# Second layer's attention, first pass over the heads: where the probabilities are multiplied by their reciprocal sum

## The chip, the cores and the metric

The kernel runs on one core of a Trainium2 chip. The metric is the device time of one execution in microseconds. The kernel before took 3354.78 us (median of 3 runs, 3352.99 to 3357.09). A core has five engines that run at the same time, each with its own list of instructions in a fixed order: TensorE (PE: matmuls, and PEld: its weight loads), VectorE (DVE), ScalarE (ACT), GpSimd (POOL) and SyncE (SP, which starts DMAs). They wait for each other by semaphores.

## The reference, cut to what matters

The program is a stack of four layers, each an attention and a feed-forward part. The change touches the attention of the second layer (`layer1_attention` in the code, since layers count from 0). It has two passes over 4 batches of 256 tokens and 16 heads of width 128: self attention over 256 keys, then attention over a context of 512 keys.

```python
def _gqa(q, k, v):
    scale = 1.0 / np.sqrt(q.shape[-1])
    scores = jnp.einsum('bsghd,btgd->bghst', q, k) * scale
    p = jax.nn.softmax(scores, axis=-1)
    return jnp.einsum('bghst,btgd->bsghd', p, v)
...
q = _ln(_fp8_linear_pertensor(ln_out, wq, wq_scale, q_in_scale).reshape(b, s, g, hpg, d), qln_w, qln_b)
k = _ln(_fp8_linear_pertensor(ln_out, wk, wk_scale, k_in_scale).reshape(b, s, g, d), kln_w, kln_b)
v = _fp8_linear_pertensor(ln_out, wv, wv_scale, v_in_scale).reshape(b, s, g, d)
core = _gqa(q, k, v).reshape(b, s, nh * d)
...
catq = _div_clamp_fp8(jnp.concatenate([core, xout], axis=-1), proj_smooth)
return jnp.einsum('bsi,oi->bso', catq, wproj) * (proj_in_scale * proj_w_scale)
```

The softmax of a row is exp(score - row maximum) divided by its sum. The kernel forms the exponentials and their sums, then multiplies the probabilities by the reciprocal of the sum.

## The kernel before, in words

**Slots.** Every engine runs the same loop over slots, `for g in range(FIRST, LAST)`. Slot g is one head of one batch: slots 0 to 63 are the first pass (4 batches of 16 heads, 256 keys), slots 64 to 127 the second (512 keys). The stages of a head are spread over three slots, so that three heads are in flight. In its part of slot g

- PE computes the scores of head g (`scores`, L1597, into banks that the exponentials of head g-1 must have left), transposes the probabilities of head g-1 (`turn`, L1606), does one projection for a later group of four heads (`unit`, L1653 for q and L1661 for k), transposes a normalised projection (`turn_unit`, L1684), projects values (`values`, L1675), weights the values of head g-1 (`weighted`, L1617) and projects the output of head g-2 (`project_out`, L1629).
- DVE takes the row maxima of head g (`maxima`, L1902), rounds the output of head g-2 to the fp8 grid (`quantize_head`: L1920, then `to_e4m3fn`, L1336 to L1342, which ends in `a_cat`), forms the reciprocals of the sums of head g (`reciprocal`, L1907), and takes mean and variance of the projection (`unit`, L1886, L1889, L1896, which ends in `a_head_var`). In slots 3, 4 and 5 of the first three batches, and slot 3 of the fourth, it also rounds the inputs of the next batch (`quantize`, L1864 to L1876, ahead of the next maxima).
- ACT copies the weighted output of head g-2 out of PSUM (`keep_out`, L1734), copies the transposed probabilities of head g-1 (`keep_turned`, L1774), takes the exponentials of head g (`exps`, L1782), normalises the projection of slot g-1 (`norm_unit`, L1742), multiplies the probabilities of head g (`scale`, L1789), and moves transposed projections and values (L1758, L1767). In some slots it starts with four products over weights (`scale_q`, L1717, L1718).
- POOL turns a variance into scale and bias (`coefs`, L1556 to L1561). In some slots it first forms the low part of the q weights (`q_low`, L1567), in others it ends with the split of the output weights (`split`, L1548, L1550).

**Four slots, one group.** Units fall in the slots whose number leaves 2, 3 or 0 when divided by 4, values in those that leave 1. `q_low` falls in slots 0, 4, 45, 49, 53 and 57 of the first pass, `split` in slots 2, 6, 10, 58 and 62.

**Buffers.** Probabilities, reciprocals and maxima have two buffers each. The semaphore `probs_ready` counts the heads whose probabilities are finished; `turn` of head g waits for g+1. In the second pass DVE does the multiplication itself (`normalize`, L1914).

Of the kernel before, what the change touches and what calls it, by code (L numbers as in the profile page):

```python
# [10 lines left out]
ALU = mybir.AluOpType  # L11
# [7 lines left out]
S = 256  # L19
# [4 lines left out]
TB = S // P  # L24
# [71 lines left out]
def rstd_gpsimd(core, g, shifted, rstd, var_ready, rstd_ready):  # L96
    g.wait_ge(var_ready, 1)
    g.tensor_tensor(rstd[:, :], shifted[:, :], core.neg_half[:, 0:NT], ALU.pow).then_inc(rstd_ready, 1)
# [217 lines left out]
def at_least(eng, sem, value):  # L316

    if isinstance(value, int) and value <= 0:
        return
    eng.wait_ge(sem, value)  # L320
# [1024 lines left out]
def layer1_attention(core):  # L1345
# [4 lines left out]
    HPQ, GPQ = 4, 2  # L1350
# [7 lines left out]
    HEADS = PASSES * H  # L1358
    KEYS = (S, C)
    SCORES, TURN, OUT, PROJECT, TURNED, SUM = 0, 2, 3, 4, 6, 7  # L1360
    with ExitStack() as ctx:
# [24 lines left out]
        probs, probs_t = sb("probs", [P, 2, TB, C]), sb("probs_t", [P, 2, CT, S])  # L1386
        neg_max, sums, recip = sb("neg_max", [P, 2, TB]), sb("sums", [P, 2, TB]), sb("recip", [P, 2, TB])
# [14 lines left out]
        scores_full, max_ready, exp_ready, recip_ready = sem("scores_full"), sem("max_ready"), sem("exp_ready"), sem("recip_ready")  # L1402
        probs_ready, turn_full, turn_ready = sem("probs_ready"), sem("turn_full"), sem("turn_ready")
# [11 lines left out]
        def pass_of(quad):  # L1415
            return quad // QUADS // B
# [41 lines left out]
        def halves(g):  # L1458

            return pass_of(g // HPQ) + 1  # L1460
# [16 lines left out]
        def q_columns(n):  # L1477
            return slice(n * QW, (n + 1) * QW)

        def split_count(p, n):  # L1480
            return 2 * (p * QUADS + n + 1)
# [9 lines left out]
        def signed_scale(which):  # L1491
            return 4 if plain(which) else scale_of(which)

        with nc.Block() as block:
# [38 lines left out]
            @block.gpsimd  # L1533
            def _(g):
                rstd_gpsimd(core, g, shifted, rstd, var_ready, rstd_ready)
                g.wait_ge(var_ready, 2)
                g.wait_ge(rstd_ready, 1)
                g.tensor_tensor(rstd[:, :], shifted[:, :], core.neg_half[:, 0:NT], ALU.pow).then_inc(rstd_ready, 1)
                g.wait_ge(rstd_ready, 2)

                def split(p, n):

                    heads = slice(n * HPQ, (n + 1) * HPQ)
                    raw = w_raw[:, n % 2, :, :]
                    g.wait_ge(PROJ_IN[n % 2], 16 * ((p * QUADS + n) // 2 + 1))
                    if p == 1:
                        g.wait_ge(sum_done, (B - 1) * H + (n + 1) * HPQ)
                    g.tensor_copy(w_parts[:, 0, heads, :], raw).then_inc(parts_step, 1)  # L1548
                    g.wait_ge(parts_step, split_count(p, n) - 1)
                    g.tensor_tensor(w_parts[:, 1, heads, :], raw, w_parts[:, 0, heads, :].bitcast(F32), ALU.subtract).then_inc(parts_step, 1)  # L1550

                def coefs(which):
                    i, kind = unit_no[which], signed_scale(which)
                    g.wait_ge(stats_ready, i + 1)
                    at_least(g, normed_ready, i - 3)
                    g.tensor_tensor(head_rstd[:, i % 4, :], head_var[:, i % 4, :], core.neg_half[:, 0:BLOCK], ALU.pow).then_inc(powers_ready, 1)  # L1556
                    g.wait_ge(powers_ready, i + 1)
                    g.tensor_tensor(head_scale[:, i % 4, :], head_rstd[:, i % 4, :], signed[:, 0, kind:kind + 1].broadcast_to([P, BLOCK]), ALU.mult)
                    g.tensor_tensor(head_var[:, i % 4, :], head_rstd[:, i % 4, :], signed[:, 1, kind:kind + 1].broadcast_to([P, BLOCK]), ALU.mult).then_inc(coefs_step, 1)
                    g.wait_ge(coefs_step, i + 1)  # L1560
                    g.tensor_tensor(head_bias[:, i % 4, :], head_moments[:, i % 4, :, 0], head_var[:, i % 4, :], ALU.mult).then_inc(head_coefs, 1)  # L1561

                g.wait_ge(coefs_ready, 1)

                def q_low(p, n):
                    g.wait_ge(q_scaled, p * QUADS + n + 1)
                    g.tensor_tensor(q_w[:, 1, :, q_columns(n)], q_raw[:, n % 2, :, :], q_w[:, 0, :, q_columns(n)].bitcast(F32),  # L1567
                                    ALU.subtract).then_inc(q_parts, 1)

                split_at = {HPQ * n - 2: (0, n) for n in range(QUADS)}  # L1570
                split_at.update({(B - 1) * H + HPQ * n + 10: (1, n) for n in range(QUADS)})
                for slot in range(FIRST, LAST):
                    if slot in q_split_at:
                        q_low(*q_split_at[slot])
                    if slot in unit_at:
                        coefs(unit_at[slot])
                    if slot in split_at:
                        split(*split_at[slot])
# [127 lines left out]
            def _(act):  # L1706
# [15 lines left out]
                for t in range(NT):  # L1722
                    act.wait_ge(token_full, t + 1)
                    for k in range(DK):
                        last = act.activation(ln_t[:, k, t * P:(t + 1) * P], core.bank(4 + t % 4)[:, k * P:(k + 1) * P], ACT.Identity,
                                              bias=cols[:, LNB + k:LNB + k + 1], scale=cols[:, LNW + k:LNW + k + 1])
# [56 lines left out]
                                              bias=neg_max[:, g % 2, t:t + 1], accum_out=sums[:, g % 2, t:t + 1])  # L1783
                    last.then_inc(exp_ready, 1)

                def scale(g):
                    act.wait_ge(recip_ready, g + 1)
                    for t in range(TB):
                        last = act.mul(probs[:, g % 2, t, 0:S], probs[:, g % 2, t, 0:S], recip[:, g % 2, t:t + 1])  # L1789
                    last.then_inc(probs_ready, 1)  # L1790

                for g in range(FIRST, LAST):
                    if g in q_split_at and g > FIRST:
                        scale_q(*q_split_at[g])
                    if 0 <= g - 2 < HEADS:
                        keep_out(g - 2)
                    late = 0 <= g < HEADS and pass_of(g // HPQ) == 0
                    if g - 1 in unit_at and not late:
                        norm_unit(unit_at[g - 1])
                    if 0 <= g - 1 < HEADS:  # L1800
                        keep_turned(g - 1, 0)
                    if 0 <= g < HEADS:
                        exps(g)
                    if g - 1 in unit_at and late:
                        norm_unit(unit_at[g - 1])
                    if late:
                        scale(g)
                    if 0 <= g - 1 < HEADS and halves(g - 1) == 2:
                        keep_turned(g - 1, 1)
                    if g - 2 in unit_at:  # L1810
                        turned(unit_at[g - 2])
                    if g in values_at:
                        keep_values(values_at[g])
# [1605 lines left out]
```

## Time and profile before

| what | value |
|---|---|
| median of 3 runs | 3354.78 us |
| profiled execution, span from first to last instruction | 3349.9 us |
| first pass over the heads, maxima of slot 0 to maxima of slot 64 | 546.42 to 910.12 us, 363.7 us |
| busy in that stretch | PE 308.85, DVE 261.29, ACT 300.93, POOL 114.90 us |
| whole span, busy | PE 85%, DVE 64%, ACT 47%, POOL 11% |

The profiled execution's own time is given only as its span. In the stretch, a slot is 5.7 us long on average. PE and ACT are both busy for more than four fifths of it, so the order of waits, and not the busy share, tells what bounds a slot. The maxima on DVE (L1902) occur once per slot and mark its start.

### The profile page before, as it was taken

The numbers are of one execution on the slowest core, as the hardware profiler recorded it, in microseconds if no ns is written. First come the engines' busy times: TensorE is split into PE (matmuls) and PEld (weight loads), VectorE is DVE, ScalarE is ACT, GpSimd is POOL, SyncE is SP. The second block draws the span as 40 slices with busy tenths as digits, with TensorE's granted clock in tenths as the row PEclk, the third lists the DMA queues.
The fourth block names the chain that finished last, engine by engine and source line by source line (L and its number), as shares of the span: only waits on it lengthen the run. The fifth ranks groups of instructions, "written<-read, shape, count | busy, mean of one in ns | idle before, by whom it ended". The sixth has DMA issues, their size and how long they took to land. (4 is left out here: it accounts for less than half of the span.)

```text
span 3349.9 us, 46674 instructions
## 1 busy us (share of the span) xinstructions
PE 2832.3 (85%) x15008; PEld 1835.0 (55%) x15010; DVE 2142.2 (64%) x5173; ACT 1559.7 (47%) x3247; POOL 376.7 (11%) x675
## 2 busy tenths in 40 slices
PE   7888995898899999638999999836599999857898
PEld 4334664777677777515777777624222223234676
DVE  5675337777666666574444444578999999677432
ACT  4452225888767777452222222213266666624221
POOL 0010004322322212010000000040300000002100
PEclk9798997999999999958999999877699999977899
DMA  1002003000000000003000000001000000020000
GB/s 57 1 2 86 0 4 123 14 1 14 14 8 1 7 1 1 23 11 126 1 1 1 0 0 0 19 5 40 0 1 1 1 1 1 1 96 2 1 0 13
DMA packets 37907, 56.93 MB, mean 17 GB/s; under 512 B 6400, under 2 KB 25792, under 8 KB 36416
## 3 DMA queue, kind: packets, MB, share of 16 engines
q1 hardware_dynamic: 37696, 54.35, 4.8%
q8 instruction: 105, 1.72, 0.2%
q14 instruction: 106, 0.87, 0.1%
HBM read 52.99 MB, written 1.05 MB: 16 GB/s over the span
## 5 line engine op out<-in xcount | busy, mean ns | idle before, releaser
L2754 ACT ACTIVATE a_exps<-psum,a_ln 128x512 f32<-128x512 f32 x512 | 315.0, 684 | 191.0 <-PE psum L2684 191.0
L2825 DVE TENSOR_REDUCE a_half_max<-psum 128x1 f32<-128x1024 f32 x256 | 311.3, 1219 | 12.5 <-PE psum L2667 5.9
L1902 DVE TENSOR_REDUCE a_neg_max<-psum 128x2 f32<-128x512 f32 (+1 forms) x128 | 122.5, 957 | 174.6 <-PE psum L1597 171.8
L1617 PE MATMUL psum<-a_probs_t,a_vals 128*128 128x256 f32 x768 | 192.0, 386 | 18.2 <-ACT a_probs_t L1774 18.1
L2684 PE MATMUL psum<-a_qs,a_ks 99*128 99x512 bf16 x512 | 173.6, 389 | 34.6 <-ACT a_exps L2754 22.8
L847 DVE SCALAR_TENSOR_TENSOR f_silu<-f_silu,psum 128x352 f32<-128x352 f32 (+2 forms) x88 | 50.4, 573 | 229.8 <-ACT f_silu L820 229.7
L1097 DVE TENSOR_REDUCE a_neg_max<-psum 128x2 f32<-128x1024 f32 x64 | 78.4, 1225 | 177.2 <-PE psum L1092 177.2
L1597 PE MATMUL psum<-a_k_t,a_q_t 128*128 128x256 f32 (+1 forms) x512 | 190.7, 496 | 0.9 <-ACT a_probs L1782 0.9
L1742 ACT ACTIVATE a_normed<-psum,a_head_bias,a_head_scale 128x128 f32<-128x128 f32 x448 | 169.4, 466 | 41.0 <-POOL a_head_bias L1561 40.7
L2869 DVE TENSOR_SCALAR a_probs<-a_exps 128x1024 bf16<-128x1024 f32 x256 | 175.1, 685 | 14.5 <-ACT a_exps L2754 14.5
L1556 POOL TENSOR_TENSOR a_head_rstd<-a_head_var,neg_half 128x4 f32<-128x4 f32 x112 | 113.9, 1017 | 596.4 <-DVE a_head_var L1896 410.9
L2667 PE MATMUL psum<-a_ks,a_qs 96*128 96x512 bf16 x512 | 164.8, 406 | 12.9 <-DVE a_half_max L2825 7.6
L1782 ACT ACTIVATE a_probs<-psum,a_neg_max 128x256 f32<-128x256 f32 (+1 forms) x256 | 147.5, 586 | 39.0 <-DVE a_neg_max L1902 38.6
L1617 PEld LDWEIGHTS psum<-a_probs_t,a_vals 128*128 128x128 f32 x768 | 139.8, 191 | 46.3 <-ACT a_probs_t L1774 30.6
L1104 ACT ACTIVATE a_probs<-psum,a_neg_max 128x512 f32<-128x512 f32 x128 | 86.8, 683 | 153.2 <-DVE a_neg_max L1097 153.2
L1250 PEld LDWEIGHTS psum<-a_w_v,a_ctx_b 128*128 128x128 f32 x1024 | 124.3, 192 | 31.5 <-issue 29.7
L1629 PE MATMUL psum<-a_w_parts,a_cat 128*128 128x256 f32 x512 | 103.4, 325 | 44.5 <-DVE a_cat L1342 43.8
L781 PE MATMUL psum<-f_w_silu,f_tile_t 128*128 128x352 f32 (+2 forms) x352 | 136.8, 511 | 3.1 <-issue 2.4
L805 PE MATMUL psum<-f_w_down,f_hid_t 128*128 128x256 f32 (+1 forms) x576 | 138.7, 380 | 0.0
L2696 PE MATMUL psum<-a_exps,a_one_row 128*17 128x512 f32 x1024 | 136.4, 605 | 0.0
L781 PE MATMUL psum<-f_w_mul,f_tile_t 128*128 128x352 f32 (+2 forms) x352 | 135.3, 507 | 0.0
L1774 ACT COPY a_probs_t<-psum 128x512 f32<-128x512 f32 x192 | 113.2, 590 | 47.1 <-PE psum L1606 43.9
(480 smaller groups left out, 6118.9 us busy)
## 6 DMA issues: line engine op xcount, KB each, us to landing
a_w_raw<-in_L_xattn_wproj_dram SPq DMA_DIRECT2D x8, 512.0 KB, 3.8
f_w_silu<-in_L_ffn_gate_dram SPq DMA_DIRECT2D x1, 2112.0 KB, 9.7
f_w_mul<-in_L_ffn_up_dram SPq DMA_DIRECT2D x1, 2112.0 KB, 14.3
a_probs<-in_ctx_t_dram SPq DMA_DIRECT2D x4, 512.0 KB, 5.1
f_w_silu<-in_L_ffn_Wu_dram SPq DMA_DIRECT2D x1, 2048.0 KB, 7.8
f_w_mul<-in_L_ffn_Wg_dram SPq DMA_DIRECT2D x1, 2048.0 KB, 12.5
f_w_down<-in_L_ffn_Wd_dram SPq DMA_DIRECT2D x1, 2048.0 KB, 17.7
a_q_raw<-in_L_xattn_wq_dram SPq DMA_DIRECT2D x4, 512.0 KB, 6.9
```

Source lines behind the costliest of these rows:

```text
L781: mm = pe.matmul(core.bank(bank)[:, 0:w], self.tile_t[:, tr, k, :], weights[:, k, first:first + w], start=(k == 0), stop=(k == DK - 1))
L805: mm = pe.matmul(core.bank(6 + tr2)[:, 0:D], self.hid_t[0:w, r, i, :], self.w_down[0:w, base + i, :], start=(c2 == 0 and i == 0), stop=(c2 ...
L1597: mm = pe.matmul(core.bank(SCORES + t)[:, 0:keys], q_t[:, quad % 2, h, t * P:(t + 1) * P], k_t[:, quad % 2, h // 2, 0:keys], start=True, s ...
L1617: mm = pe.matmul(core.bank(OUT)[:, 0:S], vals[:, quad % 2, j, (h // 2) * P:(h // 2 + 1) * P], probs_t[:, g % 2, j, :], start=(j == 0), sto ...
L1742: last = act.activation(normed[:, i % 2, j * P:(j + 1) * P], bank[:, j * P:(j + 1) * P], ACT.Identity, bias=head_bias[:, i % 4, j:j + 1], ...
L1782: last = act.activation(probs[:, g % 2, t, 0:keys], core.bank(SCORES + t)[:, 0:keys], ACT.Exp, bias=neg_max[:, g % 2, t:t + 1], accum_out= ...
L2667: mm = pe.matmul(ring(("scores", s))[:, c * BANK:(c + 1) * BANK], qs[0:KS, h * TOK + t * P:h * TOK + (t + 1) * P], ks[0:KS, h * CTX + (2 * ...
L2684: pe.matmul(core.bank(LOGITS + u), ks[0:KM, h * CTX + key * P:h * CTX + (key + 1) * P], qs[0:KM, h * TOK + c * QC:h * TOK + (c + 1) * QC], ...
L2696: pe.matmul(core.bank(OUT)[32 * u:32 * u + W, :], one_row[:, :], exps[:, (TILES_PER * g + u) % UNITS, :], start=(i == 0), stop=False, skip ...
L2754: act.activation(exps[:, n % UNITS, :], core.bank(LOGITS + u), ACT.Exp, bias=ln255[:, :]).then_inc(exp_ready, 1)
L2825: v.tensor_reduce(half_max[:, h, t, half:half + 1], ring(("scores", s)), AX.X, ALU.max, negate=True).then_inc(ring_free, 1)
L2869: v.tensor_scalar(probs[:, m % PAIRS, :], exps[:, first:first + 2, :].rearrange("p u n -> p (u n)"), ROUND, ROUND, ALU.add, ALU.subtract). ...
```

## The change

The function `scale` moves from ACT's loop to POOL's loop. On ACT it stood behind the exponentials (and behind `norm_unit`) of its own slot. On POOL it stands behind `q_low` of its slot and ahead of `coefs` and `split`. The two ACT multiplications per slot (L1789) become two POOL instructions with two operations each: a product with the reciprocal, read per partition, and a product with 1.0. The wait on `recip_ready` and the increment of `probs_ready` go with them. 64 slots, so 128 instructions.

```diff
+                def scale(slot):
+                    g.wait_ge(recip_ready, slot + 1)
+                    for t in range(TB):
+                        last = g.tensor_scalar(probs[:, slot % 2, t, 0:S], probs[:, slot % 2, t, 0:S], recip[:, slot % 2, t:t + 1], 1.0,
+                                               ALU.mult, ALU.mult)
+                    last.then_inc(probs_ready, 1)
+
                 for slot in range(FIRST, LAST):
                     if slot in q_split_at:
                         q_low(*q_split_at[slot])
+                    if 0 <= slot < HEADS and pass_of(slot // HPQ) == 0:
+                        scale(slot)
                     if slot in unit_at:
                         coefs(unit_at[slot])
...
-                def scale(g):
-                    act.wait_ge(recip_ready, g + 1)
-                    for t in range(TB):
-                        last = act.mul(probs[:, g % 2, t, 0:S], probs[:, g % 2, t, 0:S], recip[:, g % 2, t:t + 1])
-                    last.then_inc(probs_ready, 1)
-
...
-                    if late:
-                        scale(g)
```

On POOL, from the end of `coefs` of slot 10 through the split of slot 10 to `coefs` of slot 11, the kernel before has these rows (`a_w_parts` are the parts of the output weights, `a_head_rstd` the first result of `coefs`):

```order
L1561 TENSOR_TENSOR a_head_bias<-a_head_moments,a_head_var 128x4
L1548 CAST a_w_parts<-a_w_raw 128x1024
L1550 TENSOR_TENSOR a_w_parts<-a_w_raw,a_w_parts 128x1024
L1556 TENSOR_TENSOR a_head_rstd<-a_head_var,neg_half 128x4
L1558 TENSOR_TENSOR a_head_scale<-a_head_rstd,a_signed 128x4
```

and the changed kernel, in the same place on POOL, has these:

```order
L1561 TENSOR_TENSOR a_head_bias<-a_head_moments,a_head_var 128x4
L1548 CAST a_w_parts<-a_w_raw 128x1024
L1550 TENSOR_TENSOR a_w_parts<-a_w_raw,a_w_parts 128x1024
L1575 TENSOR_SCALAR a_probs<-a_probs,a_recip 128x256 x2
L1556 TENSOR_TENSOR a_head_rstd<-a_head_var,neg_half 128x4
L1558 TENSOR_TENSOR a_head_scale<-a_head_rstd,a_signed 128x4
```

The two multiplications of head 11 now stand behind the split of slot 10 and ahead of `coefs` of slot 11.

On ACT, from the exponentials of slot 27 to the start of slot 28's copies, before:

```order
L1782 ACTIVATE a_probs,a_sums<-psum,a_neg_max 128x256 x2
L1742 ACTIVATE a_normed<-psum,a_head_bias,a_head_scale 128x128 x4
L1789 ACTIVATE a_probs<-a_probs,a_recip 128x256 x2
L1734 ACTIVATE a_heads_in<-psum,a_recips 128x256
L1774 COPY a_probs_t<-psum 128x512
```

and in the changed kernel, where the same functions have moved by nine lines:

```order
L1791 ACTIVATE a_probs,a_sums<-psum,a_neg_max 128x256 x2
L1751 ACTIVATE a_normed<-psum,a_head_bias,a_head_scale 128x128 x4
L1743 ACTIVATE a_heads_in<-psum,a_recips 128x256
L1783 COPY a_probs_t<-psum 128x512
```

The copy of the weighted output (`a_heads_in`) follows the normalisation at once.

## Rows read from the trace of the kernel before

**Rows 1.** Two stretches: length, busy PE, PEld, DVE, ACT, POOL; then clock and DMA.
```profile
682.39:701.09 18.70, 17.92 (x101) 14.99 (x101) 13.14 (x56) 17.45 (x49) 4.72 (x13) 1.00 0.00 1
546.42:910.12 363.70, 308.85 (x1606) 252.92 (x1607) 261.29 (x966) 300.93 (x804) 114.90 (x220) 0.95 0.05 16
```
**Rows 2.** Waits, 545 to 905 us: waiter, waited for, us in total, times, longest.
```profile
PE psum L1629 <- DVE a_cat L1342: 41.7, 35, 4.8
...
DVE a_y L1920 <- ACT a_heads_in L1734: 12.3, 15, 2.3
PEld psum L1606 <- ACT a_probs L1789: 8.5, 18, 1.8
```
**Rows 3.** Timeline of slots 26 to 28: start us, us, engine line, [idle before].
```profile
695.02 0.16 DVE L1907 RECIPROCAL a_recip<-a_sums 128x2 f32<-128x2 f32 x1
...
696.50 0.23 DVE L1896 TENSOR_SCALAR a_head_var<-a_head_moments,a_scales 128x4 f32<-128x4 f32 x1
696.67 0.60 PE L1606 MATMUL psum<-ident,a_probs 128*128 128x128 f32 x4
...
696.87 0.69 DVE L1902 TENSOR_REDUCE a_neg_max<-psum 128x2 f32<-128x512 f32 x1
...
699.24 0.16 DVE L1907 RECIPROCAL a_recip<-a_sums 128x2 f32<-128x2 f32 x1
...
699.47 0.72 PE L1629 MATMUL psum<-a_w_parts,a_cat 128*128 128x256 f32 x4 [0.39 <-DVE a_cat L1342]
...
701.06 0.42 PEld L1606 LDWEIGHTS psum<-ident,a_probs 128*128 128x128 f32 x4 [0.41 <-ACT a_probs L1789]
```
**Rows 4.** Line L1789, which the change removes: ns min/median/max.
```profile
L1789 ACT ACTIVATE a_probs<-a_probs,a_recip x128: 491/528/581, 553.3 to 902.5; 128x256 f32<-128x256 f32 x128
```
**Rows 5.** Groups of instructions on POOL: busy us, mean ns of one.
```profile
L457 POOL TENSOR_TENSOR a_heads<-a_heads,a_recip 128x128 f32<-128x128 f32 x16 | 6.4, 403 | 242.9 <-DVE a_heads L683 242.9
...
L2616 POOL TENSOR_SCALAR a_exps<-a_exps 128x4096 f32<-128x4096 f32 x1 | 14.0, 14041 | 0.1
L2618 POOL TENSOR_SCALAR a_v_int<-a_exps 128x4096 bf16<-128x4096 f32 x1 | 3.6, 3603 | 0.1
L1219 POOL COPY a_ctx_b<-a_ctx_t 128x1024 f32 x3 | 3.1, 1042 | 448.3 <-PE psum L1250 448.3
L761 POOL COPY f_tile_t<-f_xn_t 128x256 f32 x12 | 4.8, 402 | 147.3 <-ACT f_silu L820 146.3 <-POOL f_scale_here L759 1.0
```
**Rows 6.** Timeline: POOL's long product and a DVE instruction beside it.
```profile
571.78 2.35 POOL L1567 TENSOR_TENSOR a_q_w<-a_q_raw,a_q_w 128x1024 fp32r<-128x1024 f32 x1
571.79 2.89 DVE L1340 TENSOR_TENSOR a_total<-a_y,a_step 128x512 f32<-128x512 bf16 x1
```
**Rows 7.** Timeline of slot 5: the inputs of the next batch are rounded.
```profile
585.66 0.16 DVE L1907 RECIPROCAL a_recip<-a_sums 128x2 f32<-128x2 f32 x1
585.73 0.59 DVE L1864 TENSOR_SCALAR a_clipped<-a_ln_t,a_recips 128x256 f32<-128x256 f32 x2
...
587.65 0.69 DVE L1340 TENSOR_TENSOR a_total<-a_y,a_step 128x512 f32<-128x512 bf16 x1
```
**Rows 8.** Timeline of slots 11 and 12, behind the split of slot 10.
```profile
616.74 2.43 POOL L1550 TENSOR_TENSOR a_w_parts<-a_w_raw,a_w_parts 128x1024 fp32r<-128x1024 f32 x1
...
618.33 0.86 DVE L1896 TENSOR_SCALAR a_head_var<-a_head_moments,a_scales 128x4 f32<-128x4 f32 x1
618.50 0.60 PE L1606 MATMUL psum<-ident,a_probs 128*128 128x128 f32 x4
```
**Rows 9.** Timeline of slots 0 and 1.
```profile
551.80 2.35 POOL L1567 TENSOR_TENSOR a_q_w<-a_q_raw,a_q_w 128x1024 fp32r<-128x1024 f32 x1
...
554.24 1.11 PE L1606 MATMUL psum<-ident,a_probs 128*128 128x128 f32 x4 [1.40 <-ACT a_probs L1789]
```
**Rows 10.** Timeline of slots 45 and 46, where ACT starts with four weight products.
```profile
794.65 0.16 DVE L1907 RECIPROCAL a_recip<-a_sums 128x2 f32<-128x2 f32 x1
...
796.30 1.01 PE L1606 MATMUL psum<-ident,a_probs 128*128 128x128 f32 x4
```

## The prediction

> **What bounds the kernel now.** I read the busy times by stretch first, then the waits of the first pass, then the timeline of single slots. In four undisturbed slots PE is busy for 17.92 of 18.70 us and ACT for 17.45 [rows 1]: both are nearly full, and PE has 0.78 us of idle time in four slots. Over the pass PE is busy for 308.85 of 363.70 us [rows 1]. Its largest wait is `project_out` for the rounded head, 41.7 us in 35 waits [rows 2], so behind PE stands DVE's chain: maxima, rounding, output projection, next scores. ACT comes third. DVE waits 12.3 us for ACT's copy of the output, and PE's weight loads 8.5 us for the multiplied probabilities [rows 2]. These two, some 21 us, are all that a freer ACT can give back, and most of the first lies in four slots (45, 49, 53, 57) where ACT begins with weight products.
>
> The timeline of slots 26 to 28 shows the clock of a slot [rows 3]. I write R for the start of the reciprocal. PE transposes the probabilities at R + 1.65 us (695.02 to 696.67) and, a slot later, at R + 1.82 us (699.24 to 701.06). DVE reaches the small instruction that writes `a_head_var` at R + 1.48 and the next maxima at R + 1.85. From maxima to the next R it needs 2.37 us (696.87 to 699.24), and the output projection starts 0.23 us behind R.
>
> **What is removed.** Two ACT instructions per slot, 528 ns each by the median [rows 4], overlapping to about 0.94 us. In 64 slots that is 60 us of ACT time, but little of it is on the path: in an undisturbed group of four slots I find 0.35 us (DVE waits for the copy in one slot of four).
>
> **What is added, and its price.** Two POOL instructions per slot over 128x256, fp32, in place, with two multiplications. The trace has no such row, so I bound it. Two POOL copies of 1024 and 256 columns, 1042 and 402 ns, give 0.83 ns a column and 190 ns fixed [rows 5]. From below: the TENSOR_SCALAR with minimum and maximum over 4096 columns took 3603 ns, (3603 - 190) / 4096 = 0.83 ns a column, which makes 0.40 us for 256 columns, 0.8 us for the pair. From above: the TENSOR_SCALAR with an addition and a subtraction, in place, took 14041 ns, 3.38 ns a column, which makes 1.06 us, 2.1 us for the pair. The ends differ in what the operations are, not in the kind of instruction. A product of two tensors in which one is repeated took 403 ns for 128 columns, 1.66 ns a column for a single multiplication [rows 5]. Two of them would be 3.3 ns a column, nearly the slow row. I take the slow row, 2.1 us a pair: it is the one with fp32 arithmetic, fp32 output and the same buffer for both.
>
> The Trainium skill (GPSIMD Engine Reference, section 3.1) says that a body of up to two operations is limited by its port at 1.03 cycles an element. The minimum-maximum row agrees (0.83 ns a column); the row with addition and subtraction, also two operations, took four times as long and does not. By that rule the pair would be near 0.8 us and the sum would be that of rival B below.
>
> **Who waits for it.** POOL begins 0.23 us behind R (the reciprocal's 0.16 us and the step of a semaphore), so the pair ends at R + 2.33 and the transposition can start at R + 2.4, against R + 1.65 and R + 1.82 now.
>
> DVE is held too. Beside POOL's product of 2.35 us a DVE addition that starts at the same time took 2.89 us [rows 6], while the same addition alone took 0.69 [rows 7]. The instruction that writes `a_head_var` took 0.86 us beside the split [rows 8] and 0.23 alone [rows 3]. It is due at R + 1.48, inside the pair, so it is held until R + 2.3, and the next maxima move from R + 1.85 to about R + 2.3. The period of DVE's chain in such a slot grows from 4.22 to 2.3 + 2.37 = 4.67 us.
>
> The Trainium skill (SBUF — State Buffer, section "Who interferes with whom") calls the pair of ports that the two engines share an exclusive lock, held for a whole instruction. The rows on L1340 and L1896 agree. The rule speaks against the change, since the products sit right in front of a DVE instruction that needs the lock.
>
> **The sum, in five terms.**
>
> 1. *Undisturbed groups of four slots, about 11.* Slot 26 begins 0.35 us earlier, so R = 694.67, the pair ends at 697.0, the maxima come at 696.95, the next R at 699.32 (0.08 late), the transposition at 699.32 + 2.4 = 701.7 against 701.06. That is +0.65 us, and from there PE has no idle time in which to win it back for two slots. POOL's `coefs` start later as well and meet more of DVE's rounding: I add 0.2 (an estimate from the same holding). 11 x 0.85 = +9.4 us.
> 2. *Behind a split, slots 7 and 11.* The products of head 11 stand behind L1550, which ends at 619.17 [rows 8]. They end at 619.3 + 2.1 = 621.4 and PE would have begun at 618.50: 2.8 us, twice: +5.6 us. The split of slot 2 falls into DVE's rounding, where PE waits anyway.
> 3. *Slots 3, 4 and 5 of the first three batches and slot 3 of the fourth*, in which DVE rounds the next inputs and is itself the bound. Slots 3 and 4 lose the 0.45 us of the held maxima each. In slot 5 no projection stands between the reciprocal and the rounding: L1864 starts 0.07 us behind the reciprocal's 0.16 [rows 7], and products of 2.1 us on POOL lie beside L1864 up to L1340, which starts at R + 2.0. I take 1.4 us of up to 2.1. 3 x (0.45 + 0.45 + 1.4) + 0.45 = +7.4 us.
> 4. *Slot 0.* The products stand behind `q_low`, which ends at 554.15; they end at 556.3, and PE began at 554.24 [rows 9]: +2.1 us.
> 5. *Slots 45, 49, 53 and 57.* The freed 0.94 us brings `q_low`, the copy and R forward. The transposition was at R + 1.65 [rows 10] and goes to R + 2.4. What is left is -0.2 each: -0.8 us.
>
> Sum: 9.4 + 5.6 + 7.4 + 2.1 - 0.8 = +23.7 us. The second pass and the other layers do not change. The profiled span goes from 3349.9 to 3373.6 us. The median of the runs stands 4.9 us above that span, which gives 3354.8 + 23.7 = 3378.5, told as 3379.
>
> **The rivals.**
>
> - *A. The forecast*, slow products on POOL. For it: the row of 3.38 ns a column and PE's lack of idle time. Against it: a single slow row, whose operations are others. Its own range takes 0.5 to 1.5 times the sum: 3367 to 3390.
> - *B. Fast products; ACT's relief decides.* This is the other side. At 0.40 us each the pair ends at R + 1.03, before the transposition and before `a_head_var` are due. Then the 11 groups win the 0.35 us of the copy and, I estimate, 0.17 of the 0.41 us for which PE's weight loads wait at 701.06 [rows 3] (the rest lies under the scores): -5.7. Slots 45, 49, 53 and 57 win up to 0.9 us each: -3.6. Behind the splits POOL still comes late, by 619.3 + 0.8 - 618.5 = 1.5 us, less what PE or DVE waited for anyway, +2.7 for two. Slot 0 +0.8, slot 5 +0.5 three times, +1.5. Sum -4.3 us: 3350.5. Without the two late splits and slot 5's collisions it would be 3346, faster than the 0.2% (6.7 us) that a measurement of this kernel can tell from no change. The point from which it decides is where the pair ends at R + 1.4, that is at 0.6 us an instruction. For it: the minimum-maximum row. Against it: the arithmetic row.
> - *C. In between*, 0.6 to 0.7 us an instruction: the steady groups neither win nor lose, and the splits (2 x 1.9), slot 5 (3 x 0.7) and slot 0 (1.2) cost 7.1 us and slots 45 to 57 give 3.6: 3358.
> - *D. Slow products that are hidden anyway.* PE's wait for the rounded head, 41.7 us, takes up the late transposition, since PE stood idle there; only terms 2 and 4 remain, with half of term 3: +11.4, 3366. Against it: in the undisturbed group only 0.78 us is idle.
> - *E. Worse than A.* The holding works both ways and DVE's five rounding instructions per slot are held by the later `coefs` in every slot: 48 slots x 0.45 = 21.6 us on top, at most 3400.
>
> **Chances.** A 0.52, B 0.23, C 0.07, D 0.10, E 0.08. Of A, D and E nearly all is slower by over 0.2%: 0.66. B is split, 0.11 faster and 0.12 the same; with C and some of D the same has 0.23. The range that should hold the time 8 times in 10 takes in most of B's side: 3349 to 3395.
>
> **What would show it.** Right: POOL's new line near 1.05 us an instruction; the transposition released by POOL at R + 2.4; `a_head_var` on DVE above 0.8 us in most slots; four undisturbed slots at 19.4 to 19.7 us instead of 18.70. Wrong: the new line near 0.4 us, with the transposition never waiting for POOL, or the four slots at 18.2 us. The forecast falls if the price of the product is not that of the arithmetic row, or if PE's wait for the rounded head shrinks by as much as its wait for POOL grows.

## The result and the profile after

The changed kernel takes 3347.73 us (median of 20 runs, 3337.73 to 3353.08). The kernel before, run beside it, takes 3351.88 us (20 runs, 3346.97 to 3359.49). The ratio is 0.9984, with a 95% interval of 0.9977 to 0.9991: a gain of about 4 us, less than the 0.2% named above, where 3379 us and a loss were forecast. The profiled span is 3341.7 us against 3349.9. The gain lies in the first pass over the heads: from the maxima of slot 0 to those of slot 64 it takes 356.81 us instead of 363.70 [rows 1]. The stretch before it is 1.1 us shorter; all behind it is as long as before within 0.3 us.

The products first. This is the changed kernel's group of instructions on POOL (busy us, mean ns of one, idle time before them):

```profile
L1575 POOL TENSOR_SCALAR a_probs<-a_probs,a_recip 128x256 f32<-128x256 f32 x128 | 61.0, 490 | 136.3 <-DVE a_recip L1908 136.2
```

and this is the answer on that line, which has the median and who waited for it (us, times):

```profile
L1575 POOL TENSOR_SCALAR a_probs<-a_probs,a_recip x128: 473/480/682, 553.1 to 894.7; 128x256 f32<-128x256 f32 x128
...
  PEld psum L1615: 9.2, 7
  PE psum L1615: 6.9, 4
```

A product takes 480 ns, not the 1.06 us of the forecast. Less the 190 ns fixed, that is 1.13 ns a column: between the lower bound (0.83) and the row of repeated products (1.66) [rows 5], far from 3.38. PE waits for the multiplied probabilities in 4 places of 64.

The slot shows why. Timeline of slots 27 and 28 after the change; the rows answer to [rows 3]:

```profile
702.28 0.16 DVE L1908 RECIPROCAL a_recip<-a_sums 128x2 f32<-128x2 f32 x1
...
702.54 0.93 POOL L1575 TENSOR_SCALAR a_probs<-a_probs,a_recip 128x256 f32<-128x256 f32 x2 [0.97 <-DVE a_recip L1908]
...
703.76 0.23 DVE L1897 TENSOR_SCALAR a_head_var<-a_head_moments,a_scales 128x4 f32<-128x4 f32 x1
703.93 0.60 PE L1615 MATMUL psum<-ident,a_probs 128*128 128x128 f32 x4
...
704.13 0.69 DVE L1903 TENSOR_REDUCE a_neg_max<-psum 128x2 f32<-128x512 f32 x1
```

The pair ends at R + 1.19 (703.47). `a_head_var` is due at R + 1.48, so nothing holds it, and it still takes 0.23 us. The transposition starts at R + 1.65, where it started before, and waits for nothing; the maxima start at R + 1.85, as before.

Stretches of the changed kernel (length; busy PE, PEld, DVE, ACT, POOL; clock, DMA share, GB/s): slot 46, slots 24 to 27, the whole pass, and slots 1, 6 and 7:

```profile
797.49:801.68 4.19, 4.19 (x26) 3.45 (x25) 3.60 (x16) 2.65 (x7) 0.98 (x3) 1.00 0.01 2
686.08:704.13 18.05, 17.64 (x102) 15.07 (x101) 13.09 (x55) 14.39 (x40) 8.54 (x21) 1.00 0.00 1
545.28:902.09 356.81, 303.31 (x1606) 252.46 (x1607) 261.04 (x965) 250.41 (x676) 177.41 (x348) 0.96 0.05 16
552.93:561.29 8.36, 7.19 (x26) 6.22 (x27) 0.84 (x4) 4.74 (x12) 3.49 (x9) 0.61 0.19 64
590.58:596.38 5.80, 3.15 (x12) 2.44 (x11) 3.59 (x17) 2.05 (x6) 2.17 (x5) 0.76 0.00 1
596.38:603.34 6.96, 4.20 (x22) 3.35 (x21) 6.36 (x16) 3.27 (x10) 4.65 (x7) 0.96 0.24 69
```

The kernel before, slots 46 and 1, which were not shown ahead:

```profile
796.50:802.12 5.62, 5.62 (x26) 4.87 (x25) 3.70 (x16) 4.29 (x11) 1.03 (x2) 0.71 0.00 0
554.09:560.36 6.27, 6.12 (x26) 5.45 (x27) 0.85 (x4) 5.74 (x16) 1.62 (x5) 0.73 0.25 85
```

Over the pass ACT is busy 50.5 us less and POOL 62.5 us more, for 6.9 us of time. A group of four goes from 18.70 to 18.05 us, one term of several. With a slot's length taken from its maxima to the next ones, the first pass divides like this; the first column after the names is the forecast's term, the last three are differences to the kernel before. Term 1 of the forecast was made for all 44 slots of eleven groups and stands in one row, which holds only 33, slots 2, 9, 13 and 61 to 63 among them. Two kernels of the experiments stand beside it: e_sub has slow products, e_actbusy has products of 0.48 us but leaves ACT as busy as before.

| slots | forecast | e_sub | changed kernel | e_actbusy |
|---|---|---|---|---|
| 0, 1 (behind `q_low`) | +2.1 | +2.9 | +2.1 | +2.3 |
| 3 to 5 of the first three batches, 3 of the fourth (inputs rounded) | +7.4 | +4.1 | +0.2 | +0.2 |
| 6 to 8 and 10 to 12 (around a split) | +5.6 | +11.2 | +4.5 | +3.4 |
| 59, 60 (around a split) | 0 | +3.8 | -0.6 | -0.1 |
| 45, 46, 49, 50, 53, 54, 57, 58 (ACT's weight products) | -0.8 | -3.8 | -9.5 | +0.4 |
| 38, 39, 52 | 0 | +0.2 | +1.8 | -0.2 |
| the 33 others, mostly undisturbed groups | +9.4 | +5.8 | -5.4 | -2.7 |
| sum | +23.7 | +24.2 | -6.9 | +3.3 |

How far a single slot can be trusted is seen in e_round_aa (below), whose pass has the same instructions as the changed kernel's. Its pass is 356.96 us, but slots 38 and 39 are as short in it as before the change, and slots 45 and 46 are 1.14 and 0.31 us longer than in the changed kernel. Its rows are -8.4 instead of -9.5 and +1.0 instead of +1.8; the others agree within 0.3 us.

The loss is where POOL begins late, and these rows of the changed kernel's timeline show it, first in slots 0 and 1 (they answer to [rows 9]), then behind a split in slot 12 ([rows 8]):

```profile
550.64 2.35 POOL L1567 TENSOR_TENSOR a_q_w<-a_q_raw,a_q_w 128x1024 fp32r<-128x1024 f32 x1
553.10 0.95 POOL L1575 TENSOR_SCALAR a_probs<-a_probs,a_recip 128x256 f32<-128x256 f32 x2
...
554.10 1.12 PE L1615 MATMUL psum<-ident,a_probs 128*128 128x128 f32 x4 [2.42 <-POOL a_probs L1575]
...
620.09 2.42 POOL L1550 TENSOR_TENSOR a_w_parts<-a_w_raw,a_w_parts 128x1024 fp32r<-128x1024 f32 x1
622.49 0.93 POOL L1575 TENSOR_SCALAR a_probs<-a_probs,a_recip 128x256 f32<-128x256 f32 x2
623.47 0.66 PE L1615 MATMUL psum<-ident,a_probs 128*128 128x128 f32 x4 [1.46 <-POOL a_probs L1575]
```

Part of the cost comes through the clock. In slot 1, behind the wait of 2.42 us, the granted clock is 0.61 against 0.73 before. In slot 6 it is 0.76, between full speed (2.4 GHz) and half of it, and PE had waited there for the rounded head:

```profile
593.50 1.13 PE L1638 MATMUL psum<-a_w_parts,a_cat 128*128 128x256 f32 x4 [2.65 <-DVE a_cat L1342]
```

Four such matmuls take 0.72 us elsewhere [rows 3]. The length of the wait alone doesn't decide it. In the kernel before, slot 6 had a wait of 2.12 us and kept the full clock, and in the changed kernel slot 22 has as long a wait as slot 6 at a clock of 1.00:

```profile
680.23 0.71 PE L1638 MATMUL psum<-a_w_parts,a_cat 128*128 128x256 f32 x4 [2.63 <-DVE a_cat L1342]
```

The clock also works for the change, in slots 45 to 58: slot 46 ran at a clock of 0.71 before and took 5.62 us with PE busy throughout; now it runs at 1.00 and takes 4.19. In slot 45, ahead of it, PE's wait for the rounded head is the same in both (2.24 and 2.23 us); a wait of 0.76 us for ACT's copy of the transposed probabilities is gone. That this wait held the clock down isn't shown: in e_hybrid (below) slot 45 is 7.52 us long as in the changed kernel, and slot 46 runs at 0.71 all the same:

```profile
790.81:796.42 5.61, 5.61 (x26) 4.86 (x25) 3.76 (x16) 2.76 (x7) 2.16 (x5) 0.71 0.01 1
```

Waits of the changed kernel from 540 to 905 us (waiter, waited for, us, times, longest), against [rows 2]:

```profile
PE psum L1638 <- DVE a_cat L1342: 38.9, 28, 3.0
PEld psum L1615 <- POOL a_probs L1575: 9.2, 7, 2.8
PE psum L1615 <- POOL a_probs L1575: 6.9, 4, 2.4
DVE a_y L1921 <- ACT a_heads_in L1743: 5.2, 4, 1.6
```

DVE waits 5.2 us instead of 12.3 for ACT's copy. PE's wait for the rounded head, 38.9 us, is its largest as before.

### The profile page after: what moved, and what is told of

Its sections match the earlier page's. It is cut to its first block and busy times, and to the rows that moved or that the text cites. A ratio compares the mean times of both kernels' runs of the same rounds, so it can differ in the third digit from the quotient of the medians.

```text
span 3341.7 us, 46676 instructions
## 1 busy us (share of the span) xinstructions
PE 2824.1 (85%) x15010; PEld 1834.3 (55%) x15010; DVE 2140.8 (64%) x5173; ACT 1509.0 (45%) x3119; POOL 438.9 (13%) x803
```

## Experiments

Ratios are to the kernel before, run in the same job; "pass" is the stretch from the maxima of slot 0 to those of slot 64 (363.7 us before, 356.8 changed).

### e_sub: the price step

```diff
-  g.tensor_scalar(..., recip[:, slot % 2, t:t + 1], 1.0, ALU.mult, ALU.mult)
+  g.tensor_scalar(..., recip[:, slot % 2, t:t + 1], 0.0, ALU.mult, ALU.subtract)
```

> The changed kernel with the second operation of GpSimd's products made a subtraction of 0.0 instead of a product with 1.0 (same values). Theory P (the operation sets the price: additions and subtractions run slowly, products fast): the new line goes from 0.48 us to about 1.05 us an instruction, as the row of 3.38 ns a column with addition and subtraction says, or about half of the extra if only one of two operations is slow (0.75 us). Then the pass over the heads, 356.8 us in the changed kernel, grows. Theory L (the slow row was slow because of its 4096 columns in one buffer, not because of its operations): the line stays at 0.48 us and the pass at 357 us.

Measured: 3378.49 us against 3349.17, ratio 1.0089 (1.0072 to 1.0105); pass 387.85 us. The group of instructions, two waits of PE and four undisturbed slots in this kernel:

```profile
L1575 POOL TENSOR_SCALAR a_probs<-a_probs,a_recip 128x256 f32<-128x256 f32 x128 | 146.9, 1158 | 104.3 <-DVE a_recip L1908 104.3
```

```profile
PE psum L1615 <- POOL a_probs L1575: 45.8, 41, 4.0
...
PE psum L1638 <- DVE a_cat L1342: 21.2, 13, 2.2
```

```profile
699.23:718.80 19.57, 17.87 (x100) 14.91 (x100) 13.57 (x57) 14.37 (x40) 14.12 (x21) 1.00 0.00 1
```

With a subtraction in the instruction the product takes 1158 ns instead of 490 by the mean (1145 instead of 480 by the median). The instruction has the same shape, buffers, scalars and place, so the operation alone sets the price. The forecast's world thus exists, and its sum (363.7 + 23.7 = 387.4) meets the 387.85 us. One term is met as well: an undisturbed group takes 19.57 us instead of 18.70, +0.87 where +0.85 was forecast. (The row of the 33 others has only +5.8, since it holds 33 slots and not 44, and slots 9, 13 and 63 in it are 2.5 us shorter together.) The other terms are off by 1 to 6 us in both directions. PE's wait for the products grows from 2.0 us in the kernel before to 45.8, and its wait for the rounded head falls from 41.7 [rows 2] to 21.2: nearly half of the lateness falls where PE stood idle before, which was rival D's mechanism. The difference, 23.3 us, is about what the pass grows by. A timeline of two slots of this kernel shows a step of the forecast that failed:

```profile
712.19 0.16 DVE L1908 RECIPROCAL a_recip<-a_sums 128x2 f32<-128x2 f32 x1
...
712.45 2.26 POOL L1575 TENSOR_SCALAR a_probs<-a_probs,a_recip 128x256 f32<-128x256 f32 x2 [2.55 <-DVE a_recip L1908]
...
713.69 0.37 DVE L1897 TENSOR_SCALAR a_head_var<-a_head_moments,a_scales 128x4 f32<-128x4 f32 x1
714.22 0.69 DVE L1903 TENSOR_REDUCE a_neg_max<-psum 128x2 f32<-128x512 f32 x1 [0.15 <-PE psum L1606]
...
714.76 0.66 PE L1615 MATMUL psum<-ident,a_probs 128*128 128x128 f32 x4 [0.59 <-POOL a_probs L1575]
```

The transposition is late as forecast (R + 2.57, after a wait of 0.59 us). But `a_head_var`, due inside the pair, isn't held to its end at 714.71: it runs from 713.69 to 714.06, some 0.1 us behind the start of the second product, and takes 0.37 us. The maxima here wait for the scores on PE, not for DVE's own chain; in an undisturbed group this is so in three slots of four. Over the 47 instructions of the pass that write `a_head_var` the median is 0.38 us. Five take 0.98 to 1.64 us, and these came due inside `q_low` (slot 0) or a split (slots 3, 7, 11, 59), where they are held to its end, as in slot 11:

```profile
626.71 2.34 POOL L1550 TENSOR_TENSOR a_w_parts<-a_w_raw,a_w_parts 128x1024 fp32r<-128x1024 f32 x1
627.43 1.64 DVE L1897 TENSOR_SCALAR a_head_var<-a_head_moments,a_scales 128x4 f32<-128x4 f32 x1
```

### e_round_mm and e_round_aa: which operation is slow

```diff
 # e_round_mm
-  g.tensor_scalar(v_all[:, :, :], v_all[:, :, :], ROUND, ROUND, ALU.add, ALU.subtract)
+  g.tensor_scalar(v_all[:, :, :], v_all[:, :, :], 1.0, 1.0, ALU.mult, ALU.mult)
 # e_round_aa
+  g.tensor_scalar(v_all[:, :, :], v_all[:, :, :], ROUND, -ROUND, ALU.add, ALU.add)
```

> The changed kernel with the slow row itself (4096 columns in the fourth layer's attention, in place, addition and subtraction) made two products with 1.0; it leaves out the rounding of the values. Theory P: the row falls from 14.0 us to about 3.6 us (0.83 ns a column), or to the price per column of the new line, (480 - 190) / 256 = 1.13 ns, 4.8 us. Theory L: it stays near 14 us.

> The changed kernel with the rounding of 4096 columns in the fourth layer's attention written as two additions (of the constant and of its negative) instead of an addition and a subtraction; the same values. Theory 1 (subtraction is the slow operation): the row falls from 14.0 us to about 3.6 us, and the time falls by about the 8 to 10 us by which it fell with two products. Theory 2 (additions are slow as well): it stays at 14 us and the time at 3347 us. Theory 3: half, about 7 to 9 us.

Measured: 3333.1 us in one run for e_round_mm, which leaves out the rounding of the values, pass 356.76 us; ratio 0.9979 (0.9969 to 0.9989) for e_round_aa, pass 356.96. The row in e_round_mm:

```profile
L2617 POOL TENSOR_SCALAR a_exps<-a_exps 128x4096 f32<-128x4096 f32 x1 | 3.6, 3611 | 0.1
```

and in e_round_aa:

```profile
L2617 POOL TENSOR_SCALAR a_exps<-a_exps 128x4096 f32<-128x4096 f32 x1 | 14.0, 14021 | 0.1
```

This is the very row from which the forecast took its price, in another layer, with the same buffer and shape. Two products: 3.6 us. Two additions: 14.0, as with an addition and a subtraction. So it isn't "fp32 arithmetic" that is slow in this instruction, but addition and subtraction, by a factor of 3.9 over the whole instruction. Whether one addition is enough at this size is not shown; at 256 columns one subtraction was (e_sub).

### e_double: from which length it decides

Each pair of products is done twice, the first time into columns that nothing reads.

```diff
+  for t in range(TB):
+      g.tensor_scalar(probs[:, slot % 2, t, S:C], probs[:, slot % 2, t, 0:S], recip[:, slot % 2, t:t + 1], 1.0,
+                      ALU.mult, ALU.mult)
```

> The changed kernel with GpSimd's products done twice: first two into unused columns of the same tile, then the two that count. It puts the block at 4 x 0.48 = 1.9 us, near the 2.1 us of the prediction, with nothing else changed. Theory S (only the price in the forecast was wrong, its five terms stand): the pass goes from 356.8 us to about 363.7 + 0.85 x 23.7 = 384 us and the time to about 3371 us, the transposition waits for GpSimd at 2.2 us behind the reciprocal's start, and the instruction that writes a_head_var takes over 0.6 us in most slots. Theory H (PE's wait for the rounded head takes it up): the pass stays under 366 us and the time under 3357 us.

Measured: 3362.2 us, ratio 1.0033 (1.0019 to 1.0047), pass 373.19 us, between the two expectations. `a_head_var` takes 0.23 us by the median of the 47 in the pass, and over 0.6 us in five of them only. The wait and a group of four in this kernel:

```profile
PE psum L1618 <- POOL a_probs L1578: 26.2, 37, 3.3
```

```profile
691.55:710.35 18.80, 17.89 (x100) 14.88 (x100) 13.54 (x57) 14.42 (x41) 12.51 (x30) 1.00 0.00 1
```

1.9 us of POOL per slot makes PE wait in 37 places, and still the group is only 0.10 us longer than before, 0.75 longer than in the changed kernel: its first slot grows by 0.78 (4.81 to 5.59), and the others keep their gain. Of the 16.4 us over the changed kernel 5.8 lie in the 33 other slots, 3.5 in the rounding slots, 4.7 behind the splits (59 and 60 included) and 2.6 in the slots of ACT's weight products. The expectation that a late transposition costs its whole lateness was wrong, and so was the one that it costs nothing.

### e_actbusy: is ACT's relief the gain?

ACT waits for the reciprocals and does two products of the same size as before, but from another tile into columns that nothing reads; POOL does the products that count.

```diff
+                    if late:
+                        act.wait_ge(recip_ready, g + 1)
+                        for t in range(TB):
+                            act.mul(probs[:, g % 2, t, S:C], ln_t[:, 0, t * S:(t + 1) * S], recip[:, g % 2, t:t + 1])
```

> The changed kernel with ScalarE kept as busy as before: at the old place it waits for the reciprocal and makes two products of the same size into unused columns. Theory A (the gain is ScalarE's relief: copies of output and the weight products come earlier): the gain is gone and the late products in slots 1, 4, 6, 7 and 12 stay, so the pass is 366 to 372 us against 363.7 before the change. Theory E (the gain is that the probabilities are ready earlier than ScalarE could make them): the pass stays under 360 us.

Measured: 3355.66 us, ratio 1.0021 (1.0011 to 1.0031), pass 367.03 us, in the 366 to 372 of theory A. Its group of four:

```profile
684.11:702.60 18.49, 17.69 (x102) 15.07 (x101) 13.17 (x55) 17.45 (x49) 8.55 (x21) 1.00 0.00 1
```

With ACT busy again the pass is 10.2 us longer than in the changed kernel and 3.3 us longer than before. The eight slots of ACT's weight products are back at their old lengths (+0.4 instead of -9.5). In a group of four, 0.44 of the 0.65 us goes: the slot in which DVE waited for ACT's copy is 4.64 us again instead of 4.19. The slot that begins a group keeps its gain of 0.22 us (5.03 to 4.81): that is worth the earlier probabilities, since PE's weight loads no longer wait as they did at 701.06 us [rows 3].

### e_last: the products behind POOL's other work

```diff
-                    if 0 <= slot < HEADS and pass_of(slot // HPQ) == 0:
-                        scale(slot)
                     if slot in unit_at:
                         coefs(unit_at[slot])
...
+                    if 0 <= slot < HEADS and pass_of(slot // HPQ) == 0:
+                        scale(slot)
```

> The changed kernel with the products at the end of GpSimd's slot, behind coefs and split. coefs waits for the variance (about 1.75 us behind the reciprocal's start) and takes 1.75 us, so the products end at about R + 4.5 us instead of R + 1.2, in three of four slots, and the transposition, needed at R + 1.65 to R + 2.2, waits for 2.3 us. Theory W (the place ahead of the other work is needed): the four undisturbed slots go from 18.0 to about 24 us and the pass to 440 us or more. Rival (PE's other waits take up most): under 380 us.

Measured: 3470.2 us, ratio 1.0345 (1.0328 to 1.0361). The wait and the pass:

```profile
PE psum L1615 <- POOL a_probs L1575: 129.5, 48, 6.4
```

```profile
545.98:1021.63 475.65, 334.24 (x1606) 272.79 (x1607) 267.75 (x966) 252.47 (x676) 186.63 (x348) 0.89 0.04 12
```

Four undisturbed slots take 27.6 us (slots 24 to 27), where 24 were expected. The place costs 119 us of pass with the same 128 instructions: `coefs` waits for `a_head_var` of its own slot, and behind it the products wait too, in 48 of 64 slots. POOL's order is a queue on the path, although POOL is busy for under half of the time.

### e_split: the splits out of the way

The splits of the first half of the output weights move one slot ahead (from 2, 6, 10 to 1, 5, 9), those of the second half three slots back (from 58, 62, 66, 70 to 61, 65, 69, 73).

```diff
-                split_at = {HPQ * n - 2: (0, n) for n in range(QUADS)}
-                split_at.update({(B - 1) * H + HPQ * n + 10: (1, n) for n in range(QUADS)})
+                split_at = {HPQ * n - 3: (0, n) for n in range(QUADS)}
+                split_at.update({(B - 1) * H + HPQ * n + 13: (1, n) for n in range(QUADS)})
```

> The changed kernel with the splits of the output weights moved to the slots that have no projection unit (1, 5, 9, 61, 65, 69, 73 instead of 2, 6, 10, 58, 62, 66, 70; the first to slot -3), where GpSimd has nothing behind its products. Theory Q (products queued behind a split on GpSimd cost what the forecast's second term says, by the price of 0.48 us: 1.5 us each in slots 8, 12 and 60): slots 8 and 12 fall from 4.80 and 6.09 to 4.4 and 4.6 us, slot 60 from 6.08 to 4.8, and the pass from 356.8 to about 353.5. Rival C (slot 12 and its like are long because DVE's rounding is held by the split itself, wherever the products stand): their sum stays and only moves to other slots.

Measured: 3341.65 us against 3353.73, ratio 0.9963 (0.9949 to 0.9977). The pass in this kernel:

```profile
543.93:893.78 349.85, 301.11 (x1606) 251.61 (x1607) 259.50 (x965) 250.61 (x676) 169.35 (x344) 0.96 0.04 14
```

and who still waited for the products:

```profile
L1575 POOL TENSOR_SCALAR a_probs<-a_probs,a_recip x128: 477/480/677, 550.8 to 887.0; 128x256 f32<-128x256 f32 x128
...
  PEld psum L1615: 2.3, 3
  PE psum L1615: 1.5, 1
```

Slot 12 goes from 6.09 to 4.81 us, 60 from 6.08 to 4.80, 59 from 5.30 to 4.23, 7 from 6.96 to 4.19. Slot 8 stays at 4.80, where 4.4 was expected. Slot 5 is 2.9 us longer than before the change; a split now lies beside DVE's rounding of the next inputs there. In all the pass is 7.0 us shorter than in the changed kernel, more than the 3.3 expected, and rival C (the sum only moves to other slots) is out.

Not all of this is the products' queue. Slots 11 and 63 took as long before the change (5.30 and 11.46 us) as in the changed kernel (5.30 and 11.34), and here they take 4.22 and 9.85. These 2.6 us seem to be the price of the splits themselves, wherever the products are made. No run moves the splits with the products on ACT, so how much of the 7.0 us belongs to the products on POOL is open.

### e_swap, e_both and e_hybrid: slot 0 as well

e_swap puts the products ahead of `q_low` in slots 0 and 4, e_both does that and moves the splits, e_hybrid moves the splits and leaves the products of slots 0 to 5 on ACT.

```diff
 # e_swap, e_both
-                    if slot in q_split_at:
+                    swapped = slot in (0, 4)
+                    if slot in q_split_at and not swapped:
                         q_low(*q_split_at[slot])
                     if 0 <= slot < HEADS and pass_of(slot // HPQ) == 0:
                         scale(slot)
+                    if swapped:
+                        q_low(*q_split_at[slot])
 # e_hybrid, beside the moved splits: on POOL
+                    if 6 <= slot < HEADS and pass_of(slot // HPQ) == 0:
+                        g.wait_ge(probs_ready, slot)
 # e_hybrid: on ACT
+                    if 0 <= g < 6:
+                        scale(g)
```

> The changed kernel with the products ahead of the low part of the q weights in slots 0 and 4, instead of behind it. Theory Q: in slot 0 the transposition of head 0 waits 2.42 us for products that stand behind 2.35 us of q_low; ahead of it they end at R + 1.2, 2.4 us earlier, so slots 0 and 1 lose their 2.1 us and the granted clock of slot 1 goes back from 0.61 to 0.73 or above. Rival K (slot 1 is long for other reasons, such as the first head's missing overlap): slots 0 and 1 stay at 16.0 us in sum.

> The changed kernel with both changes of place on GpSimd: splits in the slots without a projection unit, and in slots 0 and 4 the products ahead of q_low. Theory Q (both cost only by standing ahead of the products, and so add up): slots 0 and 1 at 12 us in sum instead of 14.1 with the moved splits alone, and the pass at 349.85 - 2 to 4 = 346 to 348 us, the time 2 to 4 us under that of the moved splits. Rival G (the gain in slots 0 and 1 comes back later through the granted clock, as with the exchange alone, where slots 22 and 45 became longer by 1.3 and 1.1 us): the pass at 350 us or above.

> The changed kernel with the moved splits and the products of slots 0 to 5 on ScalarE as before the change. In the changed kernel slots 0 to 5 take 45.3 us against 43.2 before the change, since the products stand behind q_low and the split, and collide with DVE's rounding in slot 5. Theory Q: the pass falls from 349.85 (moved splits alone) to 347 us. Rival G: what is won in the first slots is lost to the granted clock or to ScalarE's load, and the pass stays at 350 us.

Measured: e_swap 3341.71 us, ratio 0.9966 (0.9952 to 0.9980), pass 353.98; e_both 3338.83 us against 3349.7, 0.9964 (0.9951 to 0.9978), pass 350.16; e_hybrid 3338.9 us against 3349.7, 0.9962 (0.9948 to 0.9975), pass 350.22. Alone, the swap takes 4.1 us out of slots 0 and 1 (16.01 to 11.89), and slot 1 runs at a clock of 1.00. Of this 2.8 us are left at the end of the pass: slots 2, 8, 22 and 45 are 5.0 us longer, slots 6, 7, 38 and 39 are 3.9 us shorter. On top of the moved splits the swap brings nothing that can be told: slots 0 and 1 are 2.4 us shorter than in e_split, and the pass is no shorter. That is what rival G of both expectations said for e_both and e_hybrid. All three stand to the kernel before as e_split does, and none is better. Against the changed kernel's own ratio, 0.9984 (0.9977 to 0.9991), the intervals of e_split, e_swap and e_both just touch or overlap and that of e_hybrid ends 0.0002 below; their passes are 2.8 to 7.0 us shorter in the profiled executions.

## Why the prediction was wrong

The direction was wrong, and by one step.

1. **The price, 2.1 us a pair: wrong.** The forecast took the row of 14041 ns because it had "fp32 arithmetic, fp32 output and the same buffer". The property that mattered was one that the row names only through its line in the code: addition and subtraction. e_sub and the two rounding kernels show it from both sides. Measured: 0.93 to 0.95 us a pair. The lower bound was 0.8 us, so the range held the truth and the choice within it was poor. The row of repeated products, 1.66 ns a column, was read as support for the slow row; it was half of it. The Trainium skill (GPSIMD Engine Reference, section 3.1) has 1.03 cycles an element for a body of up to two operations, without telling operations apart. The runs agree for two products (3611 ns over 4096 columns) and disagree for additions (14021 ns).
2. **The transposition at R + 2.4: wrong through the price alone.** With slow products it was R + 2.57 (e_sub). With products of 0.48 us it stayed at R + 1.65.
3. **`a_head_var` held to the end of the pair: wrong in itself.** In e_sub its median over the pass is 0.38 us, 0.15 us more than alone, and not the 0.8 us that was to show the forecast right. Three of four maxima of an undisturbed group wait for PE's scores. The Trainium skill (SBUF — State Buffer, "Who interferes with whom") has the lock held for a whole instruction. The row at 713.69 lies inside a product of 1.14 us that ends 0.65 us later; so at least in this pairing DVE was not shut out for the whole of it. Whether it won the ports between the two products or never needed them long isn't settled. Beside a split the trace agrees: in slot 11 of e_sub the same instruction took 1.64 us, to the end of L1550.
4. **Term 1, +9.4: sign wrong by the price.** It is -0.65 us a group. With slow products it is +0.87 (e_sub), of +0.85 forecast. Rival B had -0.52 from the same rows (-5.7 for 11). e_actbusy splits the 0.65 into 0.44 for ACT's copy, forecast 0.35, and 0.22 for the earlier probabilities, forecast 0.17.
5. **Term 2, behind the splits: place right, size off.** For slow products it was +11.2 instead of +5.6, and slot 60, which I had left out, is 5.0 us longer besides. PE waits 3.7 to 3.9 us for the products there (slots 8, 12 and 60) instead of the forecast's 2.8, and then runs at a clock of 0.66, 0.81 and 0.65, which had no place in the sum. For products of 0.48 us, B's +2.7 for two splits stands against +2.1 in slots 7 and 8 and +1.6 in slots 11 and 12. The rest of the row's +4.5 is slot 6 with its clock of 0.76 (+1.3) and slot 10 (-0.3). Slot 6 isn't behind a split: e_swap and e_actbusy have late products behind the same splits and slot 6 at 4.55 and 4.53 us.
6. **Term 3, the rounding slots: small.** B said +1.5, measured +0.2. In e_sub +4.1 against +7.4.
7. **Term 4, slot 0: the number right by luck.** +2.1 forecast, +2.1 measured, but of two halves. PE's wait grew by 1.0 us (1.40 to 2.42), about what B had (+0.8) and half of the forecast's lateness, and PE was busy for 1.07 us more (6.12 to 7.19), as the clock fell from 0.73 to 0.61. With slow products it was +2.9 (e_sub).
8. **Term 5, slots 45 to 58: far too small in both.** B took the freed 0.94 us as the most that such a slot can win, -3.6. It was -9.5: -5.5 in slots 45, 49, 53 and 57 themselves (49 and 53 won 2.11 and 1.56), and -4.0 in the slots behind them (46, 50, 54, 58: -1.43, -1.19, -0.37, -0.99). In 46, 50 and 58 the granted clock went from 0.71, 0.75 and 0.77 to 1.00. The cause is ACT's relief, since e_actbusy takes all of it back. The size isn't firm: it is -8.4 in e_round_aa, -7.8 in e_split and -6.9 in e_hybrid, where the clock falls in some of these slots. The step that failed is that a slot's gain ends with the slot and with the 0.94 us.

Two sums in the text are 0.1 us off: 619.3 + 2.1 - 618.50 is 2.9 and not 2.8, and 619.3 + 0.8 - 618.5 is 1.6 and not 1.5. And 0.07 us is what L1864 starts behind the start of the reciprocal, not behind its 0.16 us [rows 7]. None of this changes the outcome.

Rival B was the mechanism. Its condition, the pair ended by R + 1.4, held. Its 3350.5 us was 4.3 us below the kernel before, and the changed kernel is about 4 us below it, which fits in part by luck: B's cost of slot 0 was too small by 1.3 us and its gain in slots 45 to 58 by 5.9 us, and the pass in the profiled execution gained 6.9 us. The right sum in e_sub is a warning: terms off by 1 to 6 us in both directions cancelled, so a total that fits doesn't show its parts.

What stays open: what the granted clock answers to in single slots. It is below 1 where slots 38, 39 and 52 are 1.8 us longer in the changed kernel (0.81 at 38, 0.83 at 39, 0.77 at 52). In e_round_aa, with the same instructions in the pass, it is 1.00 at 38 and 39 and falls to 0.85 and 0.91 at 45 and 46 instead; at 52 it is low in both (0.77 and 0.73). So the change alone doesn't place it.

## What to carry to other kernels

Before an instruction's price is taken from another row, compare the operations and not only shape, type and buffers; where two rows of one form are four times apart, the difference between them is the question to settle first. An instruction moved to a nearly idle engine joins a queue: list what stands ahead of it there in each slot, since 128 products cost -6.9 us in one place and +112 us in another. And count the slot behind the one that wins time: here it won 4.0 of 9.5 us, mostly by PE's clock. A second kernel with the same instructions in the stretch shows how firm such a number is.

## What the runs showed of the hardware

- GpSimd's two-operation instruction on fp32 takes 3.6 us for 128x4096 with two products and 14.0 us with two additions; for 128x256 with a scalar from memory, 0.48 us with two products and 1.15 us with a product and a subtraction (medians).
- A DVE instruction that takes 0.23 us alone took 0.38 us by the median of 47 in the pass of e_sub, where in most slots it came due about 0.1 us behind the start of the second of two GpSimd products of 1.14 us. Beside a single GpSimd instruction of 2.34 us it was held to that one's end, for up to 1.64 us.
- PE waits of nearly the same length went with different clocks: 2.65 us with a granted clock of 0.76 in slot 6 and 2.63 us with 1.00 in slot 22 of the changed kernel. In slot 6 four matmuls that take 0.72 us at the full clock took 1.13. With PE busy throughout, slot 46 took 5.62 us at a clock of 0.71 and 4.19 at 1.00.
